# A two-layer transformer on one core: the last two passes of the pipeline over rows rearranged

## The reference

```python
x = ln(x + attention0(x))     # 16 heads of 64 over the 256 tokens of a row, softmax(q k / 8) v
x = ln(x + experts0(x))       # router, top 2 of 8, gelu(x w1 + b) w2, hidden 256, and a shared expert
x = ln(x + attention1(x))     # "small": for each token apart, 16 heads of 8 attend to each other:
                              #   scores[h,g] = q[h].k[g] / 8; softmax over g; out[h] = sum_g w[h,g] v[g]
x = ln(x + experts1(x))       # router, top 2 of 8, gelu(x w1) w2, hidden 512, no bias
```

## Time and profile before

| | |
|---|---|
| median of three runs | 1473.27 us (1472.85 to 1474.88) |
| profiled execution | 1472.66 us, its span 1470.9 us |
| busy over the span | PE 95%, PEld 84%, DVE 64%, ACT 59%, POOL 35% |
| mean granted TensorE clock | 0.986 of full |
| iteration 16, `D0p0` to the end of `U1_15` | 1375.85 to about 1450.6 us |
| iteration 17 and the store | 1450.59 to 1470.9 us |

### The profile page before, as it was taken

The page is one execution under the profiler, slowest core; times in us unless marked ns, Lnnn a source line. Parts: engine busy times, 40 slices in busy tenths (PEclk is TensorE's granted clock), DMA queues, the critical chain, the costliest instruction groups (busy, mean ns, idle before and its releaser), DMA issues.

```text
span 1470.9 us, 34497 instructions
## 1 busy us (share of the span) xinstructions
PE 1395.0 (95%) x12096; PEld 1237.2 (84%) x12096; DVE 942.5 (64%) x2534; ACT 865.2 (59%) x2361; POOL 515.5 (35%) x415
## 2 busy tenths in 40 slices
PE   5897999999999999999999999999999999999837
PEld 4685989898898989989898898989889898988737
DVE  4456575775766667576666757677575667757482
ACT  4565756656575565657656565765757566574303
POOL 2307052350705325070532607043260704416140
PEclk9899999999999999999999999999999999999978
DMA  7000000000000000000000000000000000000000
GB/s 255 5 2 5 1 2 8 0 7 0 0 7 0 7 0 7 0 0 7 0 7 0 7 1 0 7 0 7 0 1 6 0 7 0 4 2 1 5 4 4
DMA packets 14089, 13.78 MB, mean 9 GB/s; under 512 B 1626, under 2 KB 12771, under 8 KB 13795
## 3 DMA queue, kind: packets, MB, share of 16 engines
q1 hardware_dynamic: 14050, 13.27, 2.8%
HBM read 11.17 MB, written 2.10 MB: 9 GB/s over the span
## 4 chain that ended last, share of the span: by engine, by line
PE 68%; issue 12%; DVE 10%; POOL 4%; ACT 3%; POOLq 2%; DVEq 1%; DMA 0%; SPq 0%; ACTq 0%
PE bank_F L1100 16%; PE bank_S L982 5%; PE bank_T L1011 4%; PE bank_A L1039 4%; PE bank_A L1024 3%; PE bank_T L968 3%; DVE hid L742 3%; PE bank_T L969 3%; PE bank_T L970 3%; PE bank_A L1032 3%; PE bank_A L969 3%; PE bank_A L968 3%; PE bank_A L970 3%; PE bank_F L968 2%; DVE neg_max L651 2%
## 5 line engine op out<-in xcount | busy, mean ns | idle before, releaser
L1100 PE MATMUL bank_F<-down,hid 128*128 128x128 f32 x3072 | 373.5, 277 | 16.3 <-DVE x L730 15.6
L1100 PEld LDWEIGHTS bank_F<-down,hid 128*128 128x128 f32 x3072 | 357.9, 192 | 25.5 <-DVE x L730 16.6
L543 ACT ACTIVATE probs<-bank_S,neg_max 128x256 f32<-128x256 f32 x512 | 236.0, 475 | 168.1 <-DVE neg_max L651 168.1
L651 DVE TENSOR_REDUCE neg_max<-bank_S 128x2 f32<-128x512 f32 x256 | 164.6, 684 | 72.8 <-PE bank_S L982 69.8
L471 POOL TENSOR_TENSOR hid<-hid,qkv 128x1024 f32<-128x1024 f32 x62 | 177.0, 2867 | 39.8 <-ACT hid L559 39.8
L730 DVE SCALAR_TENSOR_TENSOR x<-bank_F,gates,x 128x128 f32<-128x128 f32 x512 | 154.9, 344 | 47.8 <-PE bank_F L1100 37.6
L522 ACT ACTIVATE probsT<-bank_T 128x512 f32<-128x512 f32 x256 | 139.6, 605 | 47.0 <-PE bank_T L1011 46.9
L441 POOL TENSOR_TENSOR mean_sq<-sum_sq,one_over_d 128x2 f32<-128x2 f32 x16 | 3.2, 197 | 448.6 <-ACT h_row L517 448.6
L1011 PE MATMUL bank_T<-ident,probs 128*128 128x128 f32 x1024 | 138.2, 278 | 0.2 <-ACT probs L543 0.2
L459 POOL TENSOR_TENSOR hid<-qkv 128x1024 f32<-128x1024 f32 x47 | 112.2, 2388 | 66.7 <-ACT qkv L522 66.7
L1011 PEld LDWEIGHTS bank_T<-ident,probs 128*128 128x128 f32 x1024 | 112.2, 141 | 25.5 <-issue 21.3
(11 more groups left out here) (167 smaller groups left out, 3194.7 us busy)
## 6 DMA issues: line engine op xcount, KB each, us to landing
x_row<-in_x SPq DMA_DIRECT2D x16, 128.0 KB, 2.1
down<-in_w SPq DMA_DIRECT2D x1, 2048.0 KB, 15.2
out<-x SPq DMA_DIRECT2D x16, 128.0 KB, 1.8
hid<-in_w SPq DMA_DIRECT2D x1, 1536.0 KB, 7.8
hid<-in_rw SPq DMA_DIRECT2D x1, 1024.0 KB, 7.4
hid<-in_wv SPq DMA_DIRECT2D x1, 512.0 KB, 3.8
hid<-in_wq SPq DMA_DIRECT2D x1, 512.0 KB, 4.7
hid<-in_wk SPq DMA_DIRECT2D x1, 512.0 KB, 5.5
```

The lines of the kernel that those rows point to most:

```text
L543: ins = sc.activation(probs[:, h // 2 % 2, h % 2, t, :], unit.bank(f"S{h}")[:, t * S:(t + 1) * S], ACT.Exp, bias=neg_max[:, h, t:t + 1], a ...
L651: ve.tensor_reduce(neg_max[:, h, :], v.bank(f"S{h}")[:, :].rearrange("p (t k) -> p t k", t=NT), AX.X, ALU.max, negate=True).then_inc(max_r ...
L1100: ins = te.matmul(bank[:, (j * NT + t) * P:(j * NT + t + 1) * P], hid[:, e, k, tokens(t)], down[:, e, k, :], start=k == 0, stop=k == m - 1)
```

## The change

In iteration 15 the up products of row 14 are taken out, on TensorE and on ScalarE; `R1` of row 14 follows `X3T` at once, and the transposed row goes to `x_plus`, seen as `x3T_late`, whose last reader is done by then. Iteration 16 has an order of its own on TensorE, ScalarE, VectorE and GpSimd (`tail`). TensorE: the down products of experts 0 for row 15; six up products of row 14 (`W1_0` to `W1_5`); `X2T`, `LQ0`, `LQ1` of row 15; the other ten (`W1_6` to `W1_15`); the eight down products of row 14 as four units of two experts (`Q1p0` to `Q1p3`) in the banks S0, S1, A0 and A1; then `AOT`, `PROJ`, `X3T`, `U1_*` and `R1` of row 15. VectorE does the whole of attention 1 (`whole_scores`, `whole_values`) without GpSimd and without additions of pairs, and the eight mixes of row 14 stand behind `X3T`'s copy instead of between the steps of attention 1, starting from a copy of `x3` in `x4`. Iterations 0 to 14 and 17 keep their instructions.

```diff
@@ pe_units
+    if it == ROWS:
+        put("F", "D0p0", "D0p1", "D0p2", "WT0", "D0p3", "D0base")
+        put("G", *[f"W1_{u}" for u in range(LATE)])
+        put("F", "X2T", "LQ0", "LQ1")
+        put("G", *[f"W1_{u}" for u in range(LATE, 2 * E)])
+        put("Q", "Q1p0", "Q1p1", "Q1p2", "Q1p3")
+        put("G", "AOT", "PROJ", "X3T", "U1_0", "U1_1", "U1_2", "R1", *[f"U1_{u}" for u in range(3, 2 * E)])
+        return order
...
+    put("G", "R1", on=it == ROWS - 1)
+    b = b and it < ROWS - 1
     put("G", "U1_0", "U1_1", "U1_2", "R1", "U1_3", "U1_4", on=b)
@@ gpsimd
+            def tail(v):
+                inverse_std(v, 1, 1)
+                pool.wait_ge(ln_ready[1], v.at(1, 1, 1))
+                g.tensor_tensor(x3[:], x2[:], bproj[:, 0:1, :].broadcast_to([P, NT, D]), ALU.add).then_inc(x2plus_ready, 1)
+                inverse_std(v, 2, 1)
+                inverse_std(v, 3, 2)
@@ scalar
+            def tail(v):
+                router_exp(v, 0)
+                router_exp(v, 1)
+                copy_out(v, "WT0", gates0T, v.bank("WT0")[0:E + 1, 0:S])
+                sc.activation(table_load[:], table_load[:], ACT.Gelu)
+                for u in range(LATE):
+                    gelu1(v, u, "W1")
+                copy_out(v, "X2T", x2T[:], v.bank("X2T")[:, 0:S])
+                for t in range(NT):
+                    copy_out(v, f"LQ{t}", qkv1[:, t].rearrange("p h c d -> p (h c d)"), v.bank(f"LQ{t}")[:, 0:3 * D])
+                for u in range(LATE, 2 * E):
+                    gelu1(v, u, "W1")
+                for t in range(NT):
+                    head_exp(v, t)
+                sc.activation(table_load[:], table_load[:], ACT.Gelu)
+                for u in range(2 * E):
+                    gelu1(v, u)
@@ vector
+            def whole_scores(v, t):
+                dve.wait_ge(*v.drain(f"LQ{t}"))
+                for i in range(2):
+                    q, k = head_pairs(t, half(i))
+                    ins = ve.tensor_tensor(prod[:, t, half(i)], q, k, ALU.mult)
+                settled(dve, ins)
+                settled(dve, ve.reduce_sum(score1[:, t].rearrange("p h g -> p (h g)"), prod[:, t].rearrange("p h g d -> p (h g) d"), AX.X))
+                head_shift(v, t)
+            def whole_values(v, t):
+                for i in range(2):
+                    ins = ve.tensor_tensor(pv1[:, t, half(i)], *weights_and_values(t, i), ALU.mult)
+                settled(dve, ins)
+                settled(dve, ve.reduce_sum(ao[:, t].rearrange("p h d -> p (h d)"), pv1[:, t].rearrange("p h d g -> p (h d) g"), AX.X))
+                head_divide(v, t)
...
+            def tail(v):
+                gate(v, 0, 1)
+                for p in range(E // 2):
+                    mix(v, f"D0p{p}", 0, (2 * p, 2 * p + 1), x2, x1)
+                residual(v, "D0base", x2, x2)
+                ln_stats(v, 1, x2)
+                gate(v, 1, 2)
+                dve.wait_ge(stored, v.at(2, 16, 16))
+                settled(dve, ve.tensor_copy(x4[:], x3[:]))
+                ln_apply(v, 1, x2, 1)
+                for t in range(NT):
+                    whole_scores(v, t)
+                for t in range(NT):
+                    head_softmax_sum(v, t)
+                    whole_values(v, t)
+                transposed_out(v, "AOT", aoT[:])
+                dve.wait_ge(x2plus_ready, v.at(1, 1, 1))
+                residual(v, "PROJ", x3, x3)
+                ln_stats(v, 2, x3)
+                ln_apply(v, 2, x3, 1)
+                transposed_out(v, "X3T", x3T[:], x3T_parts)
+                for p in range(E // 2):
+                    mix(v, f"Q1p{p}", 1, (2 * p, 2 * p + 1), x4, x4)
+                ln_stats(v, 3, x4)
+                dve.wait_ge(*v.fill("R1"))
+                ve.tensor_copy(logits[1][:], v.bank("R1")[:, 0:NT * E].rearrange("p (t e) -> p t e", t=NT)).then_inc(v.drain("R1")[0], 1)
+                dve.drain()
+                route(v, 1)
+                ln_apply(v, 3, x4, 2)
@@ tensor
+                if name[:3] == "Q1p":
+                    pe.wait_ge(*v.drain(f"W1_{4 * int(name[3:]) + 3}"))
```

More of the change, by code:

```diff
@@ L452, in head_product @@
             def head_product(v):
-                for t, i in ((0, 1), (1, 0), (1, 1))[0 if v.a else 1:]:
+                for t, i in ((0, 1), (1, 0), (1, 1)):
                     if (t, i) != (1, 1):
@@ L626, in body @@
                     v_out(v, 3)
-                if v.b:
+                if v.b and v.next:
                     for u in range(2 * E):
@@ L739, in head_product @@
                 dve.wait_ge(*v.drain("LQ0"))
[L740 to L747, removed]
-                for i in range(2):
-                    ins = ve.tensor_tensor(pv1[:, 0, half(i)], *weights_and_values(0, i), ALU.mult)
-                    ins.then_inc(pv1_ready, 1)
-                    settled(dve, ins)
+                q, k = head_pairs(0, half(0))
+                settled(dve, ve.tensor_tensor(prod[:, 0, half(0)], q, k, ALU.mult))
+            def whole_scores(v, t):
+                dve.wait_ge(*v.drain(f"LQ{t}"))
+                for i in range(2):
+                    q, k = head_pairs(t, half(i))
[9 more added lines that the diff above has]
+                head_divide(v, t)
             def head_sum(v, t, i):
@@ L757, in head_sum @@
                     dve.wait_ge(prod_ready, v.at(1, NT, t + 1))
-                own = t == 0 and (i == 0 or not v.a)
-                n = DH1 if own else DH1 // 2
+                n = DH1 if (t, i) == (0, 0) else DH1 // 2
                 settled(dve, ve.reduce_sum(score1[:, t, half(i)], prod[:, t, half(i), :, 0:n], AX.X))
@@ L775, in head_mix @@
                 dve.wait_ge(pv1_ready, v.at(1, 2 * NT, 2 * t + i + 1))
-                n = NH1 // 2 if v.a and t == 0 else NH1
+                n = NH1 // 2 if t == 0 else NH1
                 settled(dve, ve.reduce_sum(ao[:, t, half(i)], pv1[:, t, half(i), :, 0:n], AX.X))
@@ L808, in transposed_out @@
                     ins = ve.tensor_copy(halves[0][:], source)
-                if xT:
-                    ins = ve.tensor_copy(xT[:], source)
+                if xT is not None:
+                    ins = ve.tensor_copy(xT, source)
                 if halves:
@@ L895, in body @@
                 if v.b:
-                    transposed_out(v, "AOT", aoT)
+                    transposed_out(v, "AOT", aoT[:])
                 if v.c:
@@ L911, in body @@
                     ln_apply(v, 2, x3, 1)
-                    transposed_out(v, "X3T", x3T, x3T_parts)
+                    transposed_out(v, "X3T", x3T[:] if v.next else x3T_late, x3T_parts)
                 if v.next:
@@ L1054, in unit @@
                 if name in ("R0", "R1"):
+                    if name == "R1" and v.it == ROWS - 1:
+                        wait_drained(v, name, "X3T")
                     for t in range(NT):
@@ L1059, in unit @@
                         else:
-                            ins = te.matmul(out, x3T[:, tokens(t)], router1[:], start=True, stop=True)
+                            ins = te.matmul(out, whole_x3T(v)[:, tokens(t)], router1[:], start=True, stop=True)
                     return ins
@@ L1073, in unit @@
                     return ins
-                if name[:3] == "U1_":
-                    u = int(name[3:])
-                    if u == 0:
+                if name[:3] in ("U1_", "W1_"):
+                    u, late = int(name[3:]), name[0] == "W"
+                    if u == 0 and not late:
                         wait_drained(v, name, "X3T")
@@ L1084, in unit @@
                         else:
-                            ins = te.matmul(out, up1_whole[:, u // 2 - SPLIT1, columns], x3T[:], start=True, stop=True)
+                            ins = te.matmul(out, up1_whole[:, u // 2 - SPLIT1, columns], x3T_late if late else x3T[:], start=True, stop=True)
                     return ins
```

38 lines of the change are left out of this document (24 added, 14 removed).

## The result

| | before | after |
|---|---|---|
| median, four runs each | 1474.08 us (1472.85 to 1477.24) | 1456.70 us (1454.80 to 1458.04) |
| ratio | | 0.9878, 95% interval 0.9858 to 0.9898 |
| span of the profiled execution | 1470.9 us | 1453.0 us |
| from X3T of row 14 (iteration 15) to the end of the span | 109.3 us | 95.1 us |

The change makes the kernel 1.2% faster; 1459.5 us was forecast. The last line of the table is the stretch on which the change acts, and is used as a measure throughout: X3T starts at 1361.61 before and at 1357.93 after, and no instruction ahead of it differs in the two programs. So 14.2 of the 17.9 us between the two spans lie in the changed stretch, and 13.75 were forecast. The other 3.7 were there before the changed code is reached (last experiment).

What follows compares the result with a forecast made beforehand. The prediction took iteration 16's chain, with attention 1 on VectorE setting its end, as the bound; 9.65 (earlier start) + 4.3 (shorter attention) - 0.2 (R1 wait) = 13.75 us less gave 1459.5 us, range 1456 to 1463.5 (8 in 10).

Steps and rivals of the forecast that it cites:

- What moves ahead: Iterations 15 to 16: without row 14's up products ahead, the gates of row 15 come 11.35 us earlier, clock full.
- rival C: Start of iteration 16: a fallen clock or late gelus cost 3 to 5 us, giving 1463; chance 10%.
- Six up products ahead of X2T: TensorE, iteration 16: with ScalarE's gelu they cost 1.7 us, so attention 1 starts 9.65 earlier.
- Attention 1 alone: VectorE, iteration 16: without GpSimd or mixes between, attention 1 takes 28.9 us instead of 33.17.
- The turns: Attention 1: VectorE and GpSimd each stand still during the other's product; a value product alone takes some 2.6 us.
- Rival A: Attention 1: value products alone are as fast as score products, saving 5.4 us, giving 1454; chance 6%.
- Rival B: Attention 1: products are long by themselves, not through GpSimd; 17 us more, giving 1476.5; chance 3%.
- The tail: AOT to the last down products: 8.41 us to the first up product, then 15.0 plus a 0.2 wait.
- the sum: Whole change: 9.65 + 4.3 - 0.2 = 13.75 us less.
- The wait for R1's bank: TensorE, iteration 16: U1_6 waits for VectorE's copy of R1, behind mixes and norm 3; costs 0.2 us.
- a wait of 2.3: U1_6 at full clock: it would wait 2.3 us for R1's copy, swallowing what the clock gives.

Runs made afterwards that it cites:

- last experiment: Both kernels timed and profiled once more, nothing changed: the kernel before 1475.94 us, the changed kernel 1456.73 us, ratio 0.9879.

## Why the prediction was right, step by step

All distances are from the start of X3T in iteration 15, or between two events.

| step | before | forecast | after |
|---|---|---|---|
| gates of row 15 | 16.59 | 11.35 earlier | 5.50, 11.09 earlier |
| first product of attention 1 | 32.24 | 9.65 earlier | 22.62, 9.62 earlier |
| first product to last division | 33.17 | 28.9 | 28.93 |
| AOT to the first up product | 8.41 | 8.41 | 8.06 |
| first up product to the last down products | 15.01 | 15.2 | 15.04 |
| last down products to the end | 20.3 | 20.3 | 20.3 |
| together | 109.3 | 13.75 less | 95.1, 14.2 less |

- **What moves ahead** was right to 0.3: VectorE sat 0.36 between the routing and the gates, for which the profile names no other engine. That the clock would stay full there was wrong; it fell for some 3 us, and only VectorE's routing hid it. That was luck: in the run with four leading products the fall cost 1.2 us, and in the second profile of the kernel before 1.4. It was a part of rival C's condition.
- **Six up products ahead of X2T** were reckoned at 1.7 us with ScalarE's gelu; 11.09 less 9.62 is 1.47. The run with sixteen confirms the size of a unit on this path.
- **Attention 1 alone** came out at 28.93 for 28.9. The turns that were read from two ends of two instructions were right, and with them the value product of 2.6, which no row showed alone. Rival A needed the step of 24 elements to cost nothing; the run with ordered values shows that this step is what costs. Rival B needed the products to be long by themselves, and they took 1.2 and 2.7. Leaving GpSimd out is hardly a gain by itself: with the mixes gone it is worth 0.7 us, and while they stand between the steps it costs 1.8. So of the 4.24 us by which attention 1 is shorter, 3.55 are the mixes.
- **The tail.** From AOT to the first up product 0.35 was won that the sum did not have: before, VectorE had idled 0.43 between the two statistics of norm 2 there, and after, it did not. The wait for R1's bank, forecast at 0.2, was none: the copy ended at 1424.03, just ahead of U1_6 at 1424.34. That a full clock would bring a wait of 2.3 there, and that this would swallow what the clock gives, was right in kind: in the two runs with TensorE kept busy the wait was 1.53, and the last stretch 94.1 with it and 92.2 without.
- **What the sum did not have** is the 3.7 us by which the changed kernel led before it reached the changed code. The median came 2.8 us below the forecast, still within the range. By the profiles 3.4 of the 3.7 arise in the first two iterations, and no step of the prediction explains them. That the stretch itself was met within 0.5 is in part luck too: the steps were off by 0.2 to 0.35, and one of them, the gates, in the other direction than the rest.

## What to carry to other kernels

When VectorE is the bound of a stretch in which TensorE idles, look first for what TensorE still does ahead of it and for foreign steps in VectorE's queue; here these two gave some 13 of the 14 us (the first product came 9.6 earlier, and the mixes had cost 3.5), and handing work from GpSimd to VectorE gave 0.7 at most. Where two engines have long durations side by side, compare the end of one's instruction with the end of the other's: here the ends followed each other by 2.62 and 2.56, which read as turns, and the product alone then took 2.67. And read the access pattern of a slow product before moving it: one copy with another order of elements was worth 6.6 us, nearly half of what the whole rearrangement brought.

## What the runs showed of the hardware

- A VectorE product of 1024 elements from two tensors took 1.2 us when it read runs of eight neighbouring elements, and 2.7 when it read one tensor with a step of 24 (96 bytes). The Trainium skill, VectorE: DVE Perf Modes, "Mode 1× (REGULAR) — the baseline", has float32 and odd strides working at one result a cycle; these runs show otherwise for this pattern. The penalty for each new 16-byte line in the Trainium skill, SBUF — State Buffer, "Door 1: The DMA port swizzle", fits in direction.
- VectorE and GpSimd stopped each other on products of two tensors, and not on sums: four value products took 10.6 us on both engines and 10.7 on VectorE, while a sum took 2.29 beside a product and alone.
- The granted clock fell in executions of the same instructions at some times and not at others: from 1361.8 to 1368.6 in the run with four leading products, from about 1361 to 1364 in the changed kernel, between 1367 and 1370 in the second profile of before, not at all in its first. It cost between nothing and 1.4 us, by what stood beside it.
